# One-core Trainium2 kernel: the convolution's fp32 products and a low-rank projection issued to four column strips of TensorE

## The chip, the cores and the metric

The kernel runs on one core of one Trainium2 chip. The metric is device time in microseconds (us) for one execution. Before the change three runs took 2049.83, 2053.85 and 2056.23 us, a median of 2053.85 us.

## The reference, cut to what matters

The input is `x` with shape (32, 64, 1024), 32 sequences of 64 rows of 1024; four blocks are added to it in turn. Block 0 sees the 64 rows as heads and the 1024 as positions; the others see them as tokens and features.

```python
# block 0: a long convolution along the last axis (u is x, L = 1024)
K = 2.0 * jnp.einsum('hn,hnl->hl', Ct, jnp.exp(P)).real
y = irfft(rfft(u, n=2 * L) * rfft(K, n=2 * L))[..., :L] + u * D[:, None]
x = x + y * mask
# blocks 1 and 2: per-sequence weight chosen by an id
x = x + jnp.einsum('bsi,boi->bso', x, weight[adapter_ids])
# block 3: gated MLP, with rank-16 adapters chosen per sequence
gate = lora_add(x @ W_gate.T, x, A_gate, B_gate)
up = lora_add(x @ W_up.T, x, A_up, B_up)
act = silu(gate) * up
down = act @ W_down.T + SCALE * (act @ A_down[id].T) @ B_down[id].T
x = x + down
```

What is computed here and touched by the change: the causal convolution of each of 64 heads (1024 positions x 32 sequences), and `act @ A_down[id].T`, which gives 16 numbers per token of each sequence, with another `A_down` per sequence.

## The kernel before, in words

Partitions hold 128 positions of the 1024; there are 8 such tiles (`LT`).

**Convolution (L2363 to L2412).** Heads are taken in pairs (`TG` = 2), four pairs to a chunk, eight chunks. Each pair needs a Toeplitz matrix `toep` that SyncE's queue loads from `kpad` in DRAM (1 MB a pair) and the inputs `u` and `urev` (256 KB each), all in rings of four. For each head, `convolve` issues eight fp32 products, one for each distance `d` between output tile and input tile: the stationary operand is a 128x128 block of `toep`, the moving one has (8 - d) x 32 columns, and the output has 128 partitions (the output positions of a tile). All eight add up in one half of a PSUM bank. `conv_done` is raised once per pair; VectorE then masks and adds the pair into `X` (L1479, L1483), and SyncE's queue reloads the ring slot. The last pair is written in three pieces by `convolve_last`. Between chunks `kernels` (L2358) forms the convolution kernel of a later chunk from eight fp32 products whose output has 32 partitions and 32 columns; VectorE and ScalarE prepare its operand `ge`.

**Blocks 1 and 2** follow (from 188 us to about 640 us), and then **block 3** in two stages of 16 sequences. A stage has 22 units of 128 hidden features (unit 0 is half a unit) and then the down projection in panels. In a unit TensorE works off a fixed list: seven sums of Strassen's scheme (`blocks`, F32R, three products per 128x128x512 block: high*high, high*low, low*high), products for the gate and up adapters (`add_ranks`), and `project_down` for the unit before. The F32R type takes fp32 data that was rounded; an exact operand is kept as a high and a low part.

**`project_down` (L2640)** computes the down adapters' projection. `adt` holds, for each of four groups of four sequences, 128 stationary columns: 64 (4 sequences x 16 ranks) of the high part and 64 of the low part. `ahl` holds the activations of the unit as high and low part. For each group the high and then the low activations of its 256 columns are multiplied, so 8 products of 128 output partitions x 256 columns. All sequences of a group meet all adapters of the group; what does not belong together is masked away at the end of the stage. The high half of `adt` and of `ahl` is written by ScalarE (L1031), the low half by VectorE (L1819): `down_ranks_lo`, `v_lo0`, `v_lo1`. At the end of a stage `lift_ranks` (ScalarE) copies the lower 64 output partitions, and VectorE's `down_ranks` adds and masks them.

The order of work on each engine is written out by hand; engines meet at semaphores (`unit_step` counts TensorE's steps of a unit, `evict` VectorE's).

Of the kernel before, what the change touches and what calls it, by code (L numbers as in the profile page):

```python
# [22 lines left out]
P = 128  # L23
# [10 lines left out]
TG = 2  # L34
# [35 lines left out]
LAST_BANKS = (3, 4, 5)  # L70
CHUNK_LINKS = 11
# [14 lines left out]
P1, P6, P2, L11, P5, AD, P7, P4, L21, L22, P3, L12 = range(1, 13)  # L86
USED = (P1, P6, P2, P5, P7, P4, P3)
(V_U2, V_G0, V_SILU0, V_U4, V_U3, V_UP1, V_UP0, V_ACT0, V_RANK1, V_LO0, V_G1, V_SILU1, V_ACT1,
 V_LO1) = range(1, 15)
# [43 lines left out]
def at_step(st, u, e):  # L133
    return u * 12 + (st * (12 * FT + 1) + e)


def emptied(st, u, v):
    return u * 14 + (st * 14 * FT + v)
# [35 lines left out]
def build(nc, ins, out):  # L174
    with ExitStack() as ctx:
# [99 lines left out]
        with placed(0) as s:  # L275
            ahl = sb(s, "ahl", [P, 2, 2, TILE], F32R)
            lt = sb(s, "lt", [P, 3, 2, 2, P], F32R)
            adraw = sb(s, "adraw", [P, SEQ, R])
            adt = sb(s, "adt", [P, GR, P], F32R)
# [148 lines left out]
        ad_lo = sem("ad_lo")  # L428
# [9 lines left out]
        td_lifted = sem("td_lifted")  # L438
        td_added = sem("td_added")
# [28 lines left out]
        def _(sp):  # L468
# [24 lines left out]
            def reload(c, k):  # L493

                q = c * PAIRS + k
                sp.wait_ge(conv_done, q - (RING - 1))
# [137 lines left out]
            def unit(st, u):  # L634

                store_acts(st, u - 1)
                next_ranks(st, u)
                sp.wait_ge(ad_lo, u + st * FT)
                load_down_ranks(st, u)
# [67 lines left out]
            for st in range(NST):  # L707
# [6 lines left out]
                sp.wait_ge(ad_lo, 1 + st * FT)  # L714
# [13 lines left out]
                sp.wait_ge(ad_lo, (st + 1) * FT - 2)  # L728
                load_down_ranks(st, FT - 2)
                store_acts(st, FT - 2)  # L730
                sp.wait_ge(ad_lo, (st + 1) * FT - 1)
# [34 lines left out]
        def _(pool):  # L766
# [46 lines left out]
            def clear(st):  # L813

                pool.memset(ahl[HALF:P].rearrange("p j h w -> p (j h w)").bitcast(F32), 0.0).then_inc(cleared, 1)
                pool.wait_ge(cleared, 2 * st + 1)
                pool.memset(tm[:, 1, 1, SPANS[0][1]:WHOLE_SPANS[0][1]].bitcast(F32), 0.0).then_inc(cleared, 1)
# [59 lines left out]
            for s in range(SEQ):  # L877
                pool.wait_ge(conv_done, 2 * s + 1)
                gather_outer(0, s, slice(0, SPLIT))
# [47 lines left out]
        def _(act):  # L927
# [182 lines left out]
            def down_ranks_hi(st, u, free):  # L1110

                act.wait_ge(adraw_in, u * 16 + (st * FT * 16 + 16))
                act.wait_ge(unit_step, free)
                copy(adt[:, :, 0:HALF].rearrange("p g (s r) -> p g s r", r=R),
                     adraw[:].rearrange("p (g s) r -> p g s r", g=GR)).then_inc(ad_hi, 1)
# [39 lines left out]
            def act_t0(st, u):  # L1155

                act.wait_ge(evict, emptied(st, u, V_ACT0))
                act.wait_ge(unit_step, at_step(st, u, AD))
                copy(ahl[:, 0, 0], s0).then_inc(act_hi, 1)

            def act_t1(st, u):

                act.wait_ge(evict, emptied(st, u, V_ACT1))
                copy(ahl[:, 1, 0], s1).then_inc(act_hi, 1)

            def half_unit(st):
# [3 lines left out]
                act.wait_ge(unit_step, at_step(st, 0, 4))  # L1170
# [3 lines left out]
                act.wait_ge(unit_step, at_step(st, 0, 12))  # L1174
# [3 lines left out]
                down_ranks_hi(st, 0, at_step(st, 0, AD))  # L1178
                act.wait_ge(evict, emptied(st, 0, V_ACT0))
                copy(ahl[0:HALF, 0, 0], s0[0:HALF]).then_inc(act_hi, 1)  # L1180
                act.wait_ge(evict, emptied(st, 0, V_ACT1))
                copy(ahl[0:HALF, 1, 0], s1[0:HALF]).then_inc(act_hi, 1)
# [6 lines left out]
            def unit(st, u):  # L1189

                if not isinstance(u, int):
                    down_ranks_hi(st, u - 1, at_step(st, u - 1, AD))
# [63 lines left out]
            def first_carry(st):  # L1256

                act.wait_ge(evict, emptied(st, FT - 1, V_LO1))
# [34 lines left out]
            def last_unit(st):  # L1293

                u = FT - 1
                down_ranks_hi(st, u - 1, at_step(st, u - 1, AD))
                cut_side_hi(st, 0)
                gate_t0(st, u)
                down_ranks_hi(st, u, at_step(st, u, AD))
# [6 lines left out]

            def lift_ranks(st):

                act.wait_ge(unit_step, at_step(st, FT, 1))
                for j in range(2):  # L1310
                    copy(tmp[HALF:P, j], ps[0:HALF, BANK_AD + j]).then_inc(td_lifted, 1)
# [22 lines left out]
            for st in range(NST):  # L1334
# [24 lines left out]
                for n in range(2, NSIDE):  # L1359
                    panel_hi(st, n)  # L1360
                    if n == 3:
                        lift_ranks(st)
# [9 lines left out]
        def _(dve):  # L1372
# [101 lines left out]
            def add_conv(c, i):  # L1474

                q = c * PAIRS + i
                dve.wait_ge(conv_done, q + 1)
# [245 lines left out]
            def add_last_conv():  # L1723
# [3 lines left out]
                for n, (e, first, end) in enumerate(((0, 0, LT), (1, 0, WK), (1, WK, LT))):  # L1727
                    if first:
                        dve.wait_ge(conv_done, H // TG)
                    else:  # L1730
                        dve.wait_ge(last_parts, n + 1)
# [187 lines left out]
            def v_u2(st, u):  # L1919
                dve.wait_ge(p1_copied, u + st * (FT - 1))  # L1920
# [51 lines left out]

            def v_lo1(st, u):
                dve.wait_ge(act_hi, u * 2 + (st * 2 * FT + 2))
                sub(ahl[:, 1, 1], s1, ahl[:, 1, 0].bitcast(F32)).then_inc(evict, 1)
# [19 lines left out]
            def half_unit(st):  # L1995
# [13 lines left out]
                mul(s1[top], bank(BANK_D)[top], s1[top]).then_inc(evict, 3)  # L2009
# [4 lines left out]
                down_ranks_lo(st, 0)  # L2014
                dve.wait_ge(act_hi, st * 2 * FT + 2)
                sub(ahl[top, 0, 1], s0[top], ahl[top, 0, 0].bitcast(F32))
                sub(ahl[top, 1, 1], s1[top], ahl[top, 1, 0].bitcast(F32)).then_inc(evict, 1)
# [21 lines left out]
                v_lo0(st, 1)  # L2039
# [7 lines left out]
                v_lo1(st, 1)  # L2047
                lo(st, 2, 6)

            def unit(st, u):  # L2050

                down_ranks_lo(st, u - 1)
# [16 lines left out]
                v_lo0(st, u)  # L2069
# [5 lines left out]
                v_lo1(st, u)  # L2075
# [174 lines left out]
            def last_unit(st):  # L2250

                u = FT - 1
                down_ranks_lo(st, u - 1)
# [4 lines left out]
                down_ranks_lo(st, u)  # L2258
# [8 lines left out]
                v_lo0(st, u)  # L2267
# [4 lines left out]
                v_lo1(st, u)  # L2272

            def down_ranks(st):

                blocks = mask[HALF:P, 0:GC].unsqueeze(1).to_broadcast([HALF, 2, GC])
                for j in range(2):
                    dve.wait_ge(td_lifted, 2 * st + j + 1)
                    add(tmp[HALF:P, j], ps[HALF:P, BANK_AD + j], tmp[HALF:P, j]).then_inc(td_added, 1)
                for j in range(2):  # L2280
                    dve.wait_ge(td_added, 2 * st + j + 1)
                    part = tmp[HALF:P, j].rearrange("p (g w) -> p g w", g=2)
                    mul(part, part, blocks).then_inc(td_part, 1)
# [65 lines left out]
        def _(pe):  # L2349
# [12 lines left out]
            def convolve(c, i, first=False):  # L2362
# [7 lines left out]
                for e in range(TG):  # L2370
# [20 lines left out]
            def convolve_last(c, i):  # L2391
# [4 lines left out]
                for n, (e, first, end) in enumerate(((0, 0, LT), (1, 0, WK), (1, WK, LT))):  # L2396
                    rows = urev[:, i % RING, e].rearrange("p l b -> p (l b)")
                    to = ps[:, LAST_BANKS[n], 0:LT * B]
                    for d in range(end):
                        l = max(first, d)  # L2400
                        last = mm(to[:, l * B:end * B], lhsT=toep[:, i % RING, e, d * P:(d + 1) * P],
                                  rhs=rows[:, (l - d) * B:(end - d) * B], start=d == 0, stop=d == end - 1)
                    last.then_inc(conv_done if first else last_parts, 1)
# [210 lines left out]
            def half_unit(st):  # L2614
# [23 lines left out]
                add_ranks(BANK_D, 1, 1, True).then_inc(unit_step, 8)  # L2638

            def project_down(st, u):  # L2640

                pe.wait_ge(ad_lo, u + (st * FT + 1))
                pe.wait_ge(evict, emptied(st, u, V_LO1))
                first = isinstance(u, int) and u == 0
                end = isinstance(u, int) and u == FT - 1
                for g in range(GR):
                    j, cols = g // 2, slice(g % 2 * GC, (g % 2 + 1) * GC)
                    to = ps[:, BANK_AD + j, cols]
                    mm(to, lhsT=adt[:, g], rhs=ahl[:, j, 0, cols], start=first and g % 2 == 0, stop=False)  # L2649
                    last = mm(to, lhsT=adt[:, g], rhs=ahl[:, j, 1, cols], start=False, stop=end and g % 2 == 1)  # L2650
                last.then_inc(unit_step, 1)
# [94 lines left out]
            def down(st):  # L2746
# [4 lines left out]
                pe.wait_ge(td_added, 2 * st + 2)  # L2751
# [88 lines left out]
```

## Time and profile before

| | before |
|---|---|
| median of three runs | 2053.85 us |
| the profiled execution | 2051.15 us |
| its span | 2049.5 us |
| granted TensorE clock, mean | 0.999 |
| TensorE busy | 2003.6 us (98%) |
| VectorE busy | 1771.9 us (86%) |
| ScalarE busy | 1007.3 us (49%) |
| DMA, mean rate | 230 GB/s |

Matmul records (PE) and weight-load records (PEld) are listed apart. An fp32 product shows as two weight loads and two matmul records, an F32R product as one of each. The duration of a matmul record holds its way through the array too; records of the same engine overlap, so what one costs in a row of many is the distance from start to start. L12 is line 12 of the kernel.

### The profile page before, as it was taken

How to read it: one execution, taken by the hardware profiler on the slowest of the kernel's cores; microseconds unless marked ns; L12 is line 12 of the kernel's file. 1: busy time of each engine (PE TensorE's matmuls, PEld its weight loads, DVE VectorE, ACT ScalarE, POOL GpSimd, SP SyncE). 2: the span in 40 equal slices, each digit the busy share in tenths (PEclk: the TensorE clock that was granted, in tenths of full speed). 3: DMA queues.
4: the chain of work that ended last, by engine and by line, in shares of the span. 5: the costliest groups of instructions: out<-in, count | busy, mean ns of one | idle time of the engine just before them, and what ended most of it. 6: DMA issues, size and time to landing. Idle time of an engine off the chain costs nothing.

```text
span 2049.5 us, 34188 instructions
## 1 busy us (share of the span) xinstructions
PE 2003.6 (98%) x10048; PEld 1701.1 (83%) x10048; DVE 1771.9 (86%) x2240; ACT 1007.3 (49%) x1259; POOL 145.0 (7%) x241
## 2 busy tenths in 40 slices
PE   4999999999999999999999999999999999999998
PEld 3999888888888788888888888888888888888887
DVE  7897999999999988888887779989888888868787
ACT  2223888888886543343443434464343443434332
POOL 3200000000003222210000020000000000000000
PEclk9999999999999999999999999999999999999999
DMA  7997999999998667754344996645344344478565
GB/s 282 372 343 295 356 347 354 363 350 361 347 361 329 178 184 210 209 166 123 107 118 145 337 303 212 211 149 143 109 123 120 107 119 113 118 240 303 194 203 190
DMA packets 263681, 471.07 MB, mean 230 GB/s; under 512 B 115462, under 2 KB 119750, under 8 KB 243910
## 3 DMA queue, kind: packets, MB, share of 16 engines
q1 hardware_dynamic: 246498, 427.58, 61.4%
q0 software_dynamic: 14944, 42.50, 6.7%
q8 instruction: 30, 0.49, 0.1%
q10 hardware_dynamic: 2180, 0.26, 0.1%
q14 instruction: 29, 0.24, 0.0%
HBM read 430.10 MB, written 63.73 MB: 241 GB/s over the span
## 4 chain that ended last, share of the span: by engine, by line
PE 85%; DVE 7%; DMA 4%; issue 2%; ACT 1%; DVEq 1%; ACTq 0%; SPq 0%
PE ps L2514 20%; PE ps L2516 19%; PE ps L2515 19%; PE ps L2376 6%; PE ps L2421 5%; PE ps L2423 5%; PE ps L2422 5%; DMA W<-in_w 3%; PE ps L2610 3%; DVE part L1708 1%; PE ps L2430 1%; PE ps L2650 1%; PE ps L2649 1%; DVE rows L1819 1%; ACT part L964 1%
## 5 line engine op out<-in xcount | busy, mean ns | idle before, releaser
L2514 PE MATMUL ps<-rows,oph 128*128 128x512 f32 x1196 | 468.4, 392 | 2.4 <-DVE opl L1819 1.6
L2516 PE MATMUL ps<-rows,opl 128*128 128x512 f32 x1196 | 466.1, 390 | 0.0
L2515 PE MATMUL ps<-rows,oph 128*128 128x512 f32 x1196 | 465.7, 389 | 0.0
L1708 DVE TENSOR_TENSOR part<-W,part 128x2048 fp32r<-128x2048 f32 x152 | 343.0, 2285 | 10.4 <-ACT part L964 9.8
L1822 DVE TENSOR_TENSOR tmp<-ps,tmp 128x512 f32<-128x512 f32 (+2 forms) x344 | 242.7, 706 | 101.8 <-PE ps L2516 53.1
L964 ACT ACTIVATE part<-W 128x2048 fp32r<-128x2048 f32 x152 | 290.9, 1916 | 78.4 <-DMA W<-in_w 56.6
L2516 PEld LDWEIGHTS ps<-rows,opl 128*128 128x128 f32 x1196 | 224.5, 188 | 49.2
L2514 PEld LDWEIGHTS ps<-rows,oph 128*128 128x128 f32 x1196 | 225.3, 188 | 44.3 <-DVE opl L1819 3.6
L2515 PEld LDWEIGHTS ps<-rows,oph 128*128 128x128 f32 x1196 | 224.8, 188 | 40.6
L2514 PE MATMUL ps<-th,wdh 128*128 128x512 f32 (+1 forms) x656 | 249.4, 380 | 2.3 <-DVE tmp L1822 1.2
L2515 PE MATMUL ps<-tl,wdh 128*128 128x512 f32 (+1 forms) x656 | 248.6, 379 | 0.0
L2516 PE MATMUL ps<-th,wdl 128*128 128x512 f32 (+1 forms) x656 | 248.5, 379 | 0.0
L1031 ACT ACTIVATE oph<-sraw 128x512 fp32r<-128x512 f32 x168 | 105.0, 627 | 274.1 <-PE ps L2516 137.5
L2421 PE MATMUL ps<-part,rh 128*128 128x512 f32 x596 | 235.4, 395 | 0.6 <-DVE part L1708 0.3
L2423 PE MATMUL ps<-part,rl 128*128 128x512 f32 x596 | 232.2, 390 | 0.0
L2422 PE MATMUL ps<-part,rh 128*128 128x512 f32 x596 | 232.1, 390 | 0.0
L2376 PE MATMUL ps<-urev,toep 128*128 128x256 f32 x992 | 146.4, 310 | 7.0 <-issue 6.9
L1031 ACT ACTIVATE wdh<-wraw 128x1024 fp32r<-128x1024 f32 (+1 forms) x66 | 66.5, 1008 | 173.3 <-PE ps L2516 169.7
L2376 PEld LDWEIGHTS ps<-urev,toep 128*128 128x128 f32 x992 | 142.1, 193 | 11.0 <-issue 7.0
L2514 PEld LDWEIGHTS ps<-th,wdh 128*128 128x128 f32 x656 | 123.4, 188 | 28.0 <-issue 2.5
L2516 PEld LDWEIGHTS ps<-th,wdl 128*128 128x128 f32 x656 | 123.4, 188 | 23.4
L2515 PEld LDWEIGHTS ps<-tl,wdh 128*128 128x128 f32 x656 | 123.4, 188 | 22.7
(284 smaller groups left out, 2951.0 us busy)
## 6 DMA issues: line engine op xcount, KB each, us to landing
W<-in_w SPq DMA_DIRECT2D x152, 1024.0 KB, 6.8
raw<-in_wgu SPq DMA_DIRECT2D x168, 256.0 KB, 3.1
traw<-kept_acts SPq DMA_DIRECT2D x78, 512.0 KB, 5.0
wraw<-in_wd SPq DMA_DIRECT2D x70, 512.0 KB
toep<-kpad SPq DMA_DIRECT2D x31, 1024.0 KB, 9.7
kept_acts<-tmp SPq DMA_DIRECT2D x84, 256.0 KB, 2.4
lraw<-picked_b SPq DMA_DIRECT2D x176, 96.0 KB, 2.1
lraw<-picked_b SPq DMA_DIRECT2D x176, 64.0 KB, 1.8
```

Source lines behind the costliest of these rows:

```text
L964: nc.scalar.activation(wh[c][:], W[:, c], ACT.Copy).then_inc(w_hi, 1)
L1031: return nc.scalar.activation(to, src, ACT.Copy)
L1708: V.tensor_tensor(out=wl[c][:], in0=W[:, c], in1=wh[c][:].bitcast(F32), op=ALU.subtract).then_inc(w_lo, 1)
L1822: return V.tensor_tensor(out=to, in0=a, in1=b, op=ALU.add)
L2376: last = mm(ps[:, i % RING, (e + 1) * LT * B - n:(e + 1) * LT * B], lhsT=toep[:, i % RING, e, d * P:(d + 1) * P], rhs=rows[:, 0:n], start= ...
L2421: mm(bank(o), lhsT=rh[:, at], rhs=wh[c][:, k], start=first, stop=False)
L2422: mm(bank(o), lhsT=rh[:, at], rhs=wl[c][:, k], start=False, stop=False)
L2423: last = mm(bank(o), lhsT=rl[:, at], rhs=wh[c][:, k], start=False, stop=end)
L2514: mm(to, lhsT=wh, rhs=mh, start=start, stop=False)
L2515: mm(to, lhsT=wh, rhs=ml, start=False, stop=False)
L2516: return mm(to, lhsT=wl, rhs=mh, start=False, stop=stop)
L2610: last = mm(ps[:, to, a:b], lhsT=lt[:, k, j, c], rhs=tm[:, j, c, at + a:at + b], start=start and k == 0, stop=stop and k == 2)
```

## The change

It does four things.

1. Each convolution product is issued as four, one for each strip `t` of 32 output positions: 32 stationary columns of the same `toep` block, the same moving columns, output partitions 32t to 32t + 31. `conv_done` and `last_parts` are raised by the last product of each strip, so they count four per pair, and their waits are multiplied by four.
2. `project_down` is done in fp32, without high and low parts: for each half `j` of the 16 sequences, four products, each of two sequences: 32 stationary columns (2 x 16 ranks), output partitions 32t to 32t + 31, moving columns the 128 of those two sequences (in unit 0 all 512 columns, which also sets the whole bank).
3. So `v_lo0`, `v_lo1`, `down_ranks_lo` and `lift_ranks` are gone; `down_ranks` masks straight from PSUM. ScalarE's copies stay (`act_in`, `adt`, now plain fp32).
4. TensorE's step `AD` is now counted by its own semaphore `ad_done` (four per unit), and `project_down` waits for ScalarE's copies only.

```diff
 def convolve(c, i, first=False):
...
                     for d in range(LT):
                         n = (LT - d) * B
-                        last = mm(ps[:, i % RING, (e + 1) * LT * B - n:(e + 1) * LT * B],
-                                  lhsT=toep[:, i % RING, e, d * P:(d + 1) * P], rhs=rows[:, 0:n],
-                                  start=d == 0, stop=d == LT - 1)
-                last.then_inc(conv_done, 1)
+                        for t in range(STRIPS):
+                            strip = slice(t * SW, (t + 1) * SW)
+                            last = mm(ps[strip, i % RING, (e + 1) * LT * B - n:(e + 1) * LT * B],
+                                      lhsT=toep[:, i % RING, e, d * P + t * SW:d * P + (t + 1) * SW],
+                                      rhs=rows[:, 0:n], start=d == 0, stop=d == LT - 1)
+                            if e == TG - 1 and d == LT - 1:
+                                last.then_inc(conv_done, 1)
...
             def project_down(st, u):
 
-                pe.wait_ge(ad_lo, u + (st * FT + 1))
-                pe.wait_ge(evict, emptied(st, u, V_LO1))
+                pe.wait_ge(ad_hi, u + (st * FT + 1))
+                pe.wait_ge(act_hi, u * 2 + (st * 2 * FT + 2))
...
-                for g in range(GR):
-                    j, cols = g // 2, slice(g % 2 * GC, (g % 2 + 1) * GC)
-                    to = ps[:, BANK_AD + j, cols]
-                    mm(to, lhsT=adt[:, g], rhs=ahl[:, j, 0, cols], start=first and g % 2 == 0, stop=False)
-                    last = mm(to, lhsT=adt[:, g], rhs=ahl[:, j, 1, cols], start=False, stop=end and g % 2 == 1)
-                last.then_inc(unit_step, 1)
+                for j in range(2):
+                    for t in range(STRIPS):
+                        s0 = j * TB + 2 * t
+                        cols = slice(0, TILE) if first else slice(t * P, (t + 1) * P)
+                        last = mm(ps[t * SW:(t + 1) * SW, BANK_AD + j, cols],
+                                  lhsT=adt[:, s0:s0 + 2].rearrange("p s r -> p (s r)"),
+                                  rhs=act_in[:, j, cols], start=first, stop=end)
+                        if j == 1:
+                            last.then_inc(ad_done, 1)
...
-            def down_ranks_lo(st, u):
-
-                dve.wait_ge(ad_hi, u + (st * FT + 1))
-                sub(adt[:, :, HALF:P].rearrange("p g (s r) -> p g s r", r=R),
-                    adraw[:].rearrange("p (g s) r -> p g s r", g=GR),
-                    adt[:, :, 0:HALF].bitcast(F32).rearrange("p g (s r) -> p g s r", r=R)).then_inc(ad_lo, 1)
...
-            def v_lo0(st, u):
-                dve.wait_ge(act_hi, u * 2 + (st * 2 * FT + 1))
-                sub(ahl[:, 0, 1], s0, ahl[:, 0, 0].bitcast(F32)).then_inc(evict, 1)
```

How TensorE's list reads at these places. First the products of one head in the convolution (stationary `toep`, moving `urev`, rows give the output's partitions x columns), before:

```order
L2376 MATMUL ps<-urev,toep 128x256
L2376 MATMUL ps<-urev,toep 128x224
L2376 MATMUL ps<-urev,toep 128x192
L2376 MATMUL ps<-urev,toep 128x160
L2376 MATMUL ps<-urev,toep 128x128
L2376 MATMUL ps<-urev,toep 128x96
L2376 MATMUL ps<-urev,toep 128x64
L2376 MATMUL ps<-urev,toep 128x32
```

and in the changed kernel, where each line stands for four products, one per strip:

```order
L2347 MATMUL ps<-urev,toep 32x256 x4
L2347 MATMUL ps<-urev,toep 32x224 x4
L2347 MATMUL ps<-urev,toep 32x192 x4
L2347 MATMUL ps<-urev,toep 32x160 x4
L2347 MATMUL ps<-urev,toep 32x128 x4
L2347 MATMUL ps<-urev,toep 32x96 x4
L2347 MATMUL ps<-urev,toep 32x64 x4
L2347 MATMUL ps<-urev,toep 32x32 x4
```

Nothing else moved there; neighbours in the list now write different strips. Second, `project_down` between its neighbours, here in the down panels after the last unit (within the units it stands between two F32R blocks in the same way), before:

```order
L2516 MATMUL ps<-th,wdl 128x512
L2649 MATMUL ps<-ahl,adt 128x256
L2650 MATMUL ps<-ahl,adt 128x256
L2649 MATMUL ps<-ahl,adt 128x256
L2650 MATMUL ps<-ahl,adt 128x256
L2649 MATMUL ps<-ahl,adt 128x256
L2650 MATMUL ps<-ahl,adt 128x256
L2649 MATMUL ps<-ahl,adt 128x256
L2650 MATMUL ps<-ahl,adt 128x256
L2514 MATMUL ps<-th,wdh 128x512
```

and in the changed kernel:

```order
L2491 MATMUL ps<-th,wdl 128x512
L2625 MATMUL ps<-act_in,adt 32x128 x8
L2489 MATMUL ps<-th,wdh 128x512
```

The place in the list is the same; eight products stay eight, of a quarter of the partitions and half the columns, in fp32.

## Rows read from the trace of the kernel before

**Rows 1.** Page, parts 1 and 4: busy time, and the chain that ended last.

```profile
PE 2003.6 (98%) x10048; PEld 1701.1 (83%) x10048; DVE 1771.9 (86%) x2240; ACT 1007.3 (49%) x1259; POOL 145.0 (7%) x241
...
PE 85%; DVE 7%; DMA 4%; issue 2%; ACT 1%; DVEq 1%; ACTq 0%; SPq 0%
```

**Rows 2.** Timeline of TensorE, convolution: start us, us, engine line operation, count.

```profile
54.66 18.59 PE L2376 MATMUL ps<-urev,toep 128*128 128x256 f32 x128
73.18 0.69 PE L2358 MATMUL ps<-ge 128*32 128x32 f32 x16
73.88 18.58 PE L2376 MATMUL ps<-urev,toep 128*128 128x256 f32 x128
```

**Rows 3.** Groups of TensorE by form, convolution: count, busy us, mean ns, idle before.

```profile
L2376 PE MATMUL ps<-urev,toep 128*128 128x224 f32 x124 | 34.0, 356 | 0.0
L2376 PE MATMUL ps<-urev,toep 128*128 128x128 f32 x124 | 24.1, 276 | 0.0
L2376 PE MATMUL ps<-urev,toep 128*128 128x32 f32 x124 | 22.5, 264 | 0.0
L2376 PE MATMUL ps<-urev,toep 128*128 128x96 f32 x124 | 22.5, 264 | 0.0
```

**Rows 4.** Timeline at the change from convolution to `kernels`, matmuls, then weight loads.

```profile
37.69 0.56 PE L2376 MATMUL ps<-urev,toep 128*128 128x64 f32 x4
38.18 0.69 PE L2358 MATMUL ps<-ge 128*32 128x32 f32 x16
38.80 0.48 PE L2376 MATMUL ps<-urev,toep 128*128 128x256 f32 x1
...
38.18 0.58 PEld L2358 LDWEIGHTS ps<-ge 128*32 128x32 f32 x16
```

**Rows 5.** Stretches: us, busy (count) of PE, PEld, DVE, ACT, POOL, clock, DMA share, GB/s.

```profile
54.00:73.20 19.20, 19.16 (x145) 18.66 (x145) 14.06 (x26) 4.51 (x6) 5.39 (x10) 1.00 0.90 323
...
sum 77.00, DVE 71.84; mean DVE 17.96
...
150.20:188.00 37.80, 37.80 (x282) 36.95 (x281) 24.08 (x35) 4.72 (x5) 2.39 (x4) 1.00 0.91 337
```

**Rows 6.** Stretch of 2.23 us within one head, TensorE alone: length, busy, clock, DMA share, GB/s.

```profile
90.07:91.70 1.63, 1.63 (x11) 1.00 1.01 415
91.70:92.29 0.59, 0.59 (x8) 1.00 1.06 417
```

**Rows 7.** Timeline of TensorE around one `project_down`.

```profile
710.23 0.39 PE L2516 MATMUL ps<-rows,opl 128*128 128x512 f32 x1
710.46 0.28 PE L2649 MATMUL ps<-ahl,adt 128*128 128x256 f32 x1
710.57 0.28 PE L2650 MATMUL ps<-ahl,adt 128*128 128x256 f32 x1
...
711.29 0.28 PE L2650 MATMUL ps<-ahl,adt 128*128 128x256 f32 x1
711.41 0.40 PE L2514 MATMUL ps<-rows,oph 128*128 128x512 f32 x1
```

**Rows 8.** One unit of block 3 as a stretch (columns as in rows 5).

```profile
796.57:818.07 21.49, 21.49 (x105) 18.12 (x104) 18.26 (x29) 8.79 (x15) 5.99 (x11) 1.00 0.70 208
```

**Rows 9.** Groups of VectorE from 700 us to the end: the subtractions for `ahl`.

```profile
L1819 DVE TENSOR_TENSOR ahl<-tmp,ahl 128x512 fp32r<-128x512 f32 (+1 forms) x86 | 59.1, 688 | 2.8 <-ACT ahl L1031 1.4
```

**Rows 10.** The longest waits of TensorE from 690 us to the end: total us, times, longest.

```profile
PE ps L2514 <- DVE tmp L1822: 1.2, 2, 0.6
PE ps L2514 <- DVE tl L1819: 1.0, 2, 0.7
```

More of the change, by code:

```diff
@@ L70 @@
 LAST_BANKS = (3, 4, 5)
+STRIPS = 4
+SW = P // STRIPS
 CHUNK_LINKS = 11
@@ L427, in build @@
         ad_hi = sem("ad_hi")
-        ad_lo = sem("ad_lo")
+        ad_done = sem("ad_done")
         sums = sem("sums")
@@ L495, in reload @@
                 q = c * PAIRS + k
-                sp.wait_ge(conv_done, q - (RING - 1))
+                sp.wait_ge(conv_done, q * STRIPS - (RING - 1) * STRIPS)
                 if k == PAIRS:
@@ L877, in _ @@
             for s in range(SEQ):
-                pool.wait_ge(conv_done, 2 * s + 1)
+                pool.wait_ge(conv_done, (2 * s + 1) * STRIPS)
                 gather_outer(0, s, slice(0, SPLIT))
@@ L1108, in ranks_hi, with down_ranks_in @@
                 copy(lt[:], lraw[:]).then_inc(lt_hi, 1)
-            def down_ranks_hi(st, u, free):
+            def down_ranks_in(st, u):
                 act.wait_ge(adraw_in, u * 16 + (st * FT * 16 + 16))
-                act.wait_ge(unit_step, free)
-                copy(adt[:, :, 0:HALF].rearrange("p g (s r) -> p g s r", r=R),
-                     adraw[:].rearrange("p (g s) r -> p g s r", g=GR)).then_inc(ad_hi, 1)
+                if st or not isinstance(u, int) or u > 0:
+                    act.wait_ge(ad_done, strips_done(st, u))
+                copy(adt[:], adraw[:]).then_inc(ad_hi, 1)
             def hi(st, u, i):
@@ L1305, in last_unit @@
                 act_t1(st, u)
[L1307 to L1311, printed above, removed]
             group_hi_of(0)
@@ L1476, in add_conv @@
                 q = c * PAIRS + i
-                dve.wait_ge(conv_done, q + 1)
+                dve.wait_ge(conv_done, q * STRIPS + STRIPS)
                 mi = masked[:, i % 2].rearrange("p e l b -> p e (l b)")
@@ L1728, in add_last_conv @@
                     if first:
-                        dve.wait_ge(conv_done, H // TG)
+                        dve.wait_ge(conv_done, H // TG * STRIPS)
                     else:
-                        dve.wait_ge(last_parts, n + 1)
+                        dve.wait_ge(last_parts, (n + 1) * STRIPS)
                     done = ps[:, LAST_BANKS[n], 0:LT * B].rearrange("p (l b) -> p l b", l=LT)[:, first:end]
@@ L2068, in unit @@
                 lo(st, u + 1, 5)
-                v_lo0(st, u)
                 v_g1(st, u)
@@ L2271, in last_unit @@
                 v_act1(st, u)
-                v_lo1(st, u)
             def down_ranks(st):
-                blocks = mask[HALF:P, 0:GC].unsqueeze(1).to_broadcast([HALF, 2, GC])
+                blocks = mask[HALF:P, 0:GC]
+                dve.wait_ge(ad_done, strips_done(st, FT))
                 for j in range(2):
[L2278 to L2283, printed above, removed]
+                    for g in range(2):
+                        cols = slice(g * GC, (g + 1) * GC)
+                        ins_ = mul(tmp[HALF:P, j, cols], ps[g * HALF:(g + 1) * HALF, BANK_AD + j, cols], blocks)
+                    ins_.then_inc(td_part, 1)
             dve.wait_ge(w_lo, base * WC + WC)
@@ L2397, in convolve_last @@
                     rows = urev[:, i % RING, e].rearrange("p l b -> p (l b)")
-                    to = ps[:, LAST_BANKS[n], 0:LT * B]
                     for d in range(end):
                         l = max(first, d)
-                        last = mm(to[:, l * B:end * B], lhsT=toep[:, i % RING, e, d * P:(d + 1) * P],
-                                  rhs=rows[:, (l - d) * B:(end - d) * B], start=d == 0, stop=d == end - 1)
-                    last.then_inc(conv_done if first else last_parts, 1)
+                        for t in range(STRIPS):
+                            strip = slice(t * SW, (t + 1) * SW)
+                            last = mm(ps[strip, LAST_BANKS[n], l * B:end * B],
+                                      lhsT=toep[:, i % RING, e, d * P + t * SW:d * P + (t + 1) * SW],
+                                      rhs=rows[:, (l - d) * B:(end - d) * B], start=d == 0, stop=d == end - 1)
+                            if d == end - 1:
+                                last.then_inc(conv_done if first else last_parts, 1)
             for c in range(NCHUNK - AHEAD, NCHUNK):
```

77 lines of the change are left out of this document (32 added, 45 removed).

## The prediction

> **What bounds the kernel now.** I read the page first, then TensorE's timeline and groups by form, then stretches, and last the waits. TensorE is busy 98% of the span, and the chain that ended last lies on it for 85% [rows 1]. So what the change does to TensorE's own list counts nearly one to one, wherever TensorE has no cover over it. In the convolution its records stand without a gap from 54 to 188 us: eight heads take 18.58 us, and the next chunk starts 19.22 us after the one before [rows 2]. One head is thus 2.30 us (a mid-chunk stretch agrees: 1.63 + 0.59 us and one record more [rows 6]). In block 3 a unit takes 21.49 us, all of it TensorE busy, with VectorE at 18.26 [rows 8], and the longest waits of TensorE after 690 us sum to about 1 us each [rows 10]. VectorE is no bound there, so the removed subtractions save nothing by themselves.
>
> **What a record costs.** Every width has 124 records for 62 heads [rows 3], so an fp32 product is two records, each with a weight load. From 224 to 128 columns the duration falls from 356 to 276 ns, 0.83 ns per column; below 128 it stops falling, 264 ns at 96 and at 32 columns alike [rows 3]. There the moving columns no longer set the pace; the load of 128 stationary columns does. The columns of a head sum to 1152 (256 + 224 + ... + 32). Streaming them twice costs 2 x 1152 x 0.83 = 1.92 us; the head takes 2.30. So 0.38 us per head, 24 us over 64 heads, is the load of weights that short products cannot hide. A load of 32 columns is cheaper: 16 of them in `kernels` span 0.58 us, of which the last one's duration is about 0.11, so one per 0.031 us [rows 4].
>
> **The convolution, changed.** Four products of 32 partitions replace one of 128: the same columns stream four times, with a quarter of the weights each. Everything hangs on how far products in different strips overlap; no row shows it, as the only strip work of the kernel before, `kernels`, uses one strip. The bounds from rows: complete overlap gives the streaming time alone, 1.92 us per head, I take 1.97 with some loss; no overlap at all gives eight records per distance, 8 x (0.83 x 1152 ns, with 0.031 us as the least for 32 columns) = 7.8 us per head. I take overlap: the four products have no operand or output partition in common that one must wait for, except the moving rows, which are only read. TensorE could then give back 0.33 x 64 = 21 us. But other bounds are near. From 54 to 150 us VectorE is busy 14.06 + 71.84 = 85.9 of 96.2 us (the second is its sum over 73.2 to 150.2 us) [rows 5], which leaves 10.3 us; the 40 heads of that stretch would ask for 13. From 150.2 to 188 us VectorE has room (24.08 of 37.80), and DMA moves 337 GB/s at a share of 0.91 [rows 5], against 415 at a share of 1.01 when it is full [rows 6]: 37.8 x 337 / 415 = 30.7 us, room for the 5.5 us that 17 heads would give. So at most 16 us; with DMA near its ceiling, a slot's reload behind the freed slot, and waits that appear when two engines are level, I take **-10 us**.
>
> **The changes of mode.** From convolution to `kernels`: the last short group ends at 38.25 by its 264 ns, so that record began at 37.98, and `kernels` starts at 38.18, 0.20 later instead of about 0.11 [rows 4]. Back: 38.18 to 38.80 is 0.62 us for 16 records of 0.031 (0.50) [rows 4], 0.12 more, of which I count 0.10. So about 0.1 us each way when TensorE goes between 128 and 32 columns. The 15 changes around `kernels` vanish: **-1.4 us**. Each of the 44 `project_down` now gets two: +0.2 us each, counted below.
>
> **`project_down`, changed.** Before: 710.46 to 711.41, 0.95 us, eight records at 0.12 [rows 7]. After: eight fp32 products of 128 columns, 16 records. With overlap, the four strips of a half take 2 x 128 x 0.83 = 0.21 us, both halves 0.43; 16 loads at 0.031 one after another take 0.50, and I take that, plus 0.2 for the changes of mode: 0.70. So -0.25 us in 42 units, -10.5 us. In unit 0 of each stage the products are 512 wide: 2 x 2 x 0.83 x 512 = 1.7 + 0.2 us, +0.95 twice, +1.9. Together **-8.6 us**, all on the path, since a unit is TensorE's time alone. No overlap: 16 x 0.106 + 0.2 - 0.95 = +0.95 us per unit, +40, and +12 for the wide ones.
>
> **The rest.** VectorE loses 86 subtractions of 0.69 us [rows 9] and 44 short ones, under cover of TensorE [rows 8]; nothing. If that cover went (TensorE faster by 3 us per unit), they would count. ScalarE's copies stay. `project_down` waits one engine earlier than before, behind it nothing new queues. The extra raises of `conv_done` and `ad_done` I put at nothing. The removed lift sits between panels, whose waits sum to 1 us [rows 10].
>
> Sum: -10 - 1.4 - 8.6 = -20 us against the profiled execution's 2051.15 (span 2049.5), 2031. That execution lies 2.7 us under the median of the runs, so I forecast **2034 us**.
>
> **A rule against it.** The Trainium skill (TensorE: Matmul & The Clock Gate, Packing small matmuls) says that matmuls start and end strictly in program order, and that three column tiles with 512 moving columns ran 2.38 times as fast; the same page has loads overlap running matmuls only for different row groups, which strips of the same 128 rows are not. No row here shows strips side by side. On the loads the trace disagrees already: loads run under matmuls of the same rows (PEld busy 1701 beside PE 2004 us [rows 1]). What the order rule would do here is the second rival.
>
> **The rivals.**
> 1. *Records start one per 0.031 us, whatever the strip.* For: that is the pace in `kernels` [rows 4], on one strip. Then a distance takes at least 8 x 0.031 = 0.25 us, which binds at 128 columns and fewer. The wide four (832 columns) stream 2 x 0.83 x 832 ns = 1.38 us, the narrow four take 1.0: 2.39 us per head, +0.09 x 64 = +6. With -10 from the other two terms that is -4: 2050 us, no change that counts.
> 2. *The second record of a product holds up the strips behind it (ends slower).* An fp32 product's two records use the same strip [rows 3]. If the second one waits at the head of the list until the first has streamed, then only it and the next strip's first record overlap. A head costs 4 x 1152 x 0.83 = 3.8, with 0.063 as the least for a product 4.0 us: +1.71 x 64 = +109. `project_down`: 8 x 0.106 + 0.2 = 1.05, +0.1 in 42 units (+4), in the wide ones 8 x 0.42 + 0.2 - 0.95 = +2.6 twice (+5). Less 1.4: +117, **2171 us**. It decides if a strip cannot hold one record in waiting. Against it: overlap of neighbours is then still seen. The order rule of the Trainium skill above is what would make it so.
> 3. *No overlap.* (7.8 - 2.3) x 64 + 52 - 1.4 = +403, 2457 us. For: in `kernels` every start lies behind the one before; against: only one strip is used there.
> 4. Something else, either way.
>
> **Chances.** Overlap 0.48; first rival 0.12; second 0.26; third 0.10; other 0.04. "Same" is within 0.3% (6 us), about what a measurement of this kernel can tell from no change. Of the forecast's 0.48, 0.03 falls within it (VectorE or DMA take all): faster 0.46, same 0.13 (with most of rival 1), slower 0.41. The likeliest case alone runs from 2018 (-16, -1.4 and strips' loads side by side, -0.32 x 42) to 2048. The range has to take in rival 2, up to 2180, and leaves rival 3 and the odd case out: 2018 to 2180.
>
> **What would show it.** Right: in TensorE's timeline a chunk's convolution takes 16 to 17.5 us instead of 18.58, with small waits for VectorE or DMA; starts of strips t and t + 1 lie far closer than their streaming time; a unit takes 21.25 us; granted clock stays at 1.00 (2.4 GHz). Rival 1: a chunk at 19, a unit at 21.25. Rival 2: a chunk near 32 us, a unit at 21.6. Rival 3: a chunk near 62 us, a unit at 22.4. The forecast is wrong if a chunk exceeds 18.6 us.

## The result, and the profile after

The changed kernel takes 2058.44 us (median of 20 runs, 2055.24 to 2063.47) against 2053.57 us for the kernel before in 20 runs beside it: ratio 1.0029, 95% interval 1.0023 to 1.0035. That is 5 us slower, right at the bound of 0.3%; the forecast was 20 us faster. The profiled execution has a span of 2054.8 us, 5.3 more than before.

From the profile page of the changed kernel, part 1 and the instruction queue of part 3 (packets, MB, share):

```profile
PE 1986.0 (97%) x13496; PEld 1642.7 (80%) x13496; DVE 1704.9 (83%) x2108; ACT 1009.1 (49%) x1255; POOL 142.5 (7%) x241
...
q8 instruction: 42, 0.69, 0.1%
```

TensorE is busy 17.6 us less than before [rows 1], with a third more records, and still the span is longer. The queue q8 carries instructions, in pieces of 16 KB; before, the same line had 30 packets and 0.49 MB.

TensorE's timeline in the convolution, changed kernel (start us, us, engine line operation, count, idle before with what ended it):

```profile
51.41 2.22 PE L2347 MATMUL ps<-urev,toep 128*32 128x32 f32 x67 [2.91 <-issue]
53.69 0.66 PE L2327 MATMUL ps<-ge 128*32 128x32 f32 x15
...
57.42 4.13 PE L2347 MATMUL ps<-urev,toep 128*32 128x96 f32 x127 [1.25 <-issue]
63.75 8.06 PE L2347 MATMUL ps<-urev,toep 128*32 128x96 f32 x254 [2.19 <-issue]
74.21 2.51 PE L2347 MATMUL ps<-urev,toep 128*32 128x128 f32 x87 [2.41 <-issue]
...
77.37 15.93 PE L2347 MATMUL ps<-urev,toep 128*32 128x256 f32 x512 [0.16 <-issue]
96.21 0.69 PE L2327 MATMUL ps<-ge 128*32 128x32 f32 x16 [2.91 <-DVE ge L1462]
96.96 17.59 PE L2347 MATMUL ps<-urev,toep 128*32 128x256 f32 x512
116.21 0.69 PE L2327 MATMUL ps<-ge 128*32 128x32 f32 x16 [1.66 <-DVE ge L1462]
116.96 15.93 PE L2347 MATMUL ps<-urev,toep 128*32 128x256 f32 x512
...
172.46 5.97 PE L2347 MATMUL ps<-urev,toep 128*32 128x192 f32 x128 [2.73 <-issue]
178.70 4.31 PE L2347 MATMUL ps<-urev,toep 128*32 128x192 f32 x127 [0.26 <-issue]
...
199.43 2.09 PE L2422 MATMUL ps<-part,rh 128*128 128x512 f32 x8 [0.82 <-ACT rh L986]
```

Read three things. First, eight heads in 15.93 us, 1.99 per head, where [rows 2] had 18.58: the strips do overlap. Second, idle put down to "issue", in the middle of a head, where the list has no semaphore; many of the stretches between the gaps have 127, 128 or 254 records. Third, waits for VectorE's `ge` at the end of each chunk in the loop. Blocks 1 and 2 begin at 199.43 us; before, their first product was at 188.24, so the convolution lost 11.2 us:

```profile
188.24 2.09 PE L2447 MATMUL ps<-part,rh 128*128 128x512 f32 x8
```

TensorE's waits from 32 to 200 us (total us, times, longest), changed kernel, and then before:

```profile
PE ps L2347 <- issue: 17.3, 11, 2.9
PE ps L2327 <- DVE ge L1462: 8.0, 4, 2.9
```

```profile
PE ps L2358 <- DVE ge L1465: 1.3, 1, 1.3
```

Before, there was none for issue. The stretches of the whole convolution (us, busy and count of PE, PEld, DVE, ACT, POOL, clock, DMA share, GB/s), after, and then before:

```profile
32.00:199.00 167.00, 141.03 (x4236) 121.13 (x4228) 127.17 (x220) 31.57 (x41) 25.66 (x45) 0.97 0.89 323
```

```profile
32.00:188.00 156.00, 154.54 (x1143) 150.22 (x1142) 125.99 (x219) 31.75 (x41) 25.94 (x45) 1.00 0.94 345
```

TensorE works 13.5 us less and stands 24.5 us more: +11. The granted clock is 0.97, not 1.00: three times it fell to its lower level, each time just after a wait. One wait, of 2.91 us, ends at 96.2 us; the stretches that follow it (TensorE at 1.2 GHz where the clock column says 0.50):

```profile
96.20:98.00 1.80, 1.72 (x32) 1.30 (x36) 1.73 (x5) 0.37 (x1) 0.60 (x1) 0.84 1.04 410
98.00:100.00 2.00, 2.00 (x37) 1.61 (x32) 1.93 (x3) 1.28 (x1) 0.00 (x0) 0.50 1.01 404
100.00:102.00 2.00, 2.00 (x56) 1.57 (x52) 1.93 (x3) 0.00 (x0) 0.00 (x0) 0.79 1.05 400
```

That chunk took 17.59 us where its neighbour takes 15.93, so the drop cost 1.7 us, and as much again at 172.46 (5.97 against 4.31 us for 128 records). A third drop follows the gap before 185.74 (0.60 from 185.7 to 190 us). Not every gap has one: after the 2.91 us before 51.41 and the 2.41 before 74.21 the clock stayed at 1.00.

The account of the convolution: eight chunks at 2.65 us less would be 21.2 us, and it ended 11.2 later, so 32.4 us are to be found. Issue took 17.3, the waits for `ge` 6.7 more than before, the two drops of the clock that can be read off 3.3, and a wait for ScalarE at its end 0.8. The other 4 us, with the third drop in them, were not taken apart.

The projection, changed kernel, and one unit as a stretch:

```profile
825.37 0.39 PE L2491 MATMUL ps<-rows,opl 128*128 128x512 f32 x1
825.69 0.64 PE L2625 MATMUL ps<-act_in,adt 128*32 128x128 f32 x16
826.26 0.50 PE L2489 MATMUL ps<-rows,oph 128*128 128x512 f32 x1
826.60 0.40 PE L2490 MATMUL ps<-rows,oph 128*128 128x512 f32 x1
...
804.34:825.69 21.35, 21.35 (x114) 17.46 (x113) 16.75 (x26) 8.90 (x14) 6.48 (x12) 1.00 0.73 204
```

Against [rows 7] and [rows 8], a unit is 0.14 us shorter. Sixteen records take from 825.69 to 826.26, 0.57 us, instead of 0.95; but the first one starts 0.32 after its wide neighbour instead of 0.23 (0.09 more), and the second wide record after it comes 0.34 us later, where 0.23 is the pace of such records: 0.11 more. Together that is 0.18 us less, of which the unit shows 0.14. Narrowing to 825.80 to 825.815 us shows four records in flight:

```profile
825.69 0.32 PE L2625 MATMUL ps<-act_in,adt 128*32 128x128 f32 x4
```

Each lasts 0.30 us and all four together 0.32, so they started within 0.02 us of each other.

The balance: +11.2 at the start of blocks 1 and 2, +10.6 at the first projection (694.98 against 684.41 us), +5.5 after the 22 of stage 0, +4.0 after those of stage 1, +5.3 at the end. Block 3 gave back 5.3 us net. It won 2.1 us between the first two calls of the projection and 5.9 in the 40 units that follow the second call of either stage; it lost 1.0 at the wide projection of stage 1, 0.4 between the stages and 1.3 after the last call. The convolution took 11.2.

### The profile page after: what moved, and what is told of

It reads as the page before. It is cut to its first block, busy times and chain, and to the rows that moved or that the text cites. A ratio compares the mean times of both kernels' runs of the same rounds, so it can differ in the third digit from the quotient of the medians.

```text
span 2054.8 us, 40994 instructions
## 1 busy us (share of the span) xinstructions
PE 1986.0 (97%) x13496; PEld 1642.7 (80%) x13496; DVE 1704.9 (83%) x2108; ACT 1009.1 (49%) x1255; POOL 142.5 (7%) x241
## 3 DMA queue, kind: packets, MB, share of 16 engines
q10 hardware_dynamic: 2180, 0.26, 0.1%
## 4 chain that ended last, share of the span: by engine, by line
PE 85%; DVE 9%; issue 3%; DMA 2%; ACT 1%; SPq 0%; DVEq 0%; ACTq 0%
PE ps L2489 19%; PE ps L2490 19%; PE ps L2491 19%; PE ps L2396 6%; PE ps L2398 6%; PE ps L2397 6%; PE ps L2347 3%; PE ps L2585 3%; PE ps L2405 2%; PE ps L2625 1%; DVE rows L1816 1%; DVE X L1480 1%; DVE masked L1476 1%; DMA traw<-kept_acts 1%; DVE rraw L1816 1%
## 5 line engine op out<-in xcount | busy, mean ns | idle before, releaser
L1819 DVE TENSOR_TENSOR tmp<-ps,tmp 128x512 f32<-128x512 f32 (+1 forms) x340 | 240.3, 707 | 165.0 <-PE ps L2491 89.0
L2491 PEld LDWEIGHTS ps<-rows,opl 128*128 128x128 f32 x1196 | 224.5, 188 | 50.1
L2347 PE MATMUL ps<-urev,toep 128*32 128x256 f32 (+7 forms) x3968 | 134.1, 296 | 24.6 <-issue 24.4
L2347 PEld LDWEIGHTS ps<-urev,toep 128*32 128x32 f32 x3968 | 114.1, 114 | 44.2 <-issue 28.9
```

Of the source, the lines that this page charges most:

```text
L1819: return V.tensor_tensor(out=to, in0=a, in1=b, op=ALU.add)
L2347: last = mm(ps[strip, i % RING, (e + 1) * LT * B - n:(e + 1) * LT * B], lhsT=toep[:, i % RING, e, d * P + t * SW:d * P + (t + 1) * SW], rh ...
L2491: return mm(to, lhsT=wl, rhs=mh, start=False, stop=stop)
```

## The experiments

The question after the first look: what is the idle put down to issue? Theory F: TensorE's code, which comes in pieces and arrives too late. Each product of a head became four, so a pair has 256 instructions (64 products, each two loads and two matmuls) instead of 64. The 12 pieces more on q8 were there to be explained too, and 128 records between two gaps are 256 instructions with their loads. Ten kernels ran.

### Each part alone

`e1_projection_only` keeps the convolution's whole products:

```diff
-                        for t in range(STRIPS):
...
+                        last = mm(ps[:, i % RING, (e + 1) * LT * B - n:(e + 1) * LT * B],
+                                  lhsT=toep[:, i % RING, e, d * P:(d + 1) * P], rhs=rows[:, 0:n],
+                                  start=d == 0, stop=d == LT - 1)
+                last.then_inc(conv_done, STRIPS)
```

> The projection in strips, the convolution as before (whole products, conv_done raised by four at once). Both theories: units 21.35 us as in the changed kernel instead of 21.49, blocks 1 and 2 starting at 188 us as before; 2051 - 6 = about 2047 us, ratio 0.997. If the projection's strips disturbed something outside their own unit, the ratio would be 1.000 or above.

Measured: 2047.22 us, ratio 0.9975 (0.9962 to 0.9988); blocks 1 and 2 start at 188.71 us. As expected: this part alone is a gain.

`e2_conv_only` is the kernel before with `convolve` and `convolve_last` of the change.

> The convolution in strips, the projection as before. Theory F (TensorE's straight-line code arrives too late): blocks 1 and 2 start near 199 us as in the changed kernel, units 21.49, total about +11 us, ratio 1.005. Rival V (VectorE's slower preparation of ge in this build, by whatever reason lies in the other part of the change): the start would be near 190 us and the ratio about 1.000.

Measured: 2065.09 us, ratio 1.0066 (1.0053 to 1.0080), blocks 1 and 2 at 198.12 us, 13.3 us of idle by issue and 10.6 by `ge` after the first product. The loss is the convolution's alone; rival V, a slower VectorE by reason of the other part, fell. The two parts add up to +0.4%, near the 1.0029 of both.

### The loop written out

`e3_unrolled`, and the same edit in the kernel before as `e4_before_unrolled`:

```diff
-            with pe.Fori(1, NCHUNK - AHEAD) as c:
+            for c in range(1, NCHUNK - AHEAD):
```

> The changed kernel with the loop over chunks 1 to 5 written out, so that no code is run twice: 16 more pairs are read for the first time. Theory F: idle of TensorE put down to issue in the convolution grows from 17 us (after the first product) to 30 to 40 us, in all chunks and not only in the first and last; about 16 more pieces on the instruction queue q8; ratio to the kernel before 1.008 to 1.015. Rival D (the stalls come from the data: toeplitz loads, PSUM or SBUF taken by others) : no change against the changed kernel, 1.003.

> Control: the kernel before with the same loop written out, 4 KB of TensorE code per pair instead of 16. Theory F: about 4 to 5 more pieces on q8, no issue idle worth naming, 1.000 +- 0.001. If writing out the loop costs by itself (register work, something else), it shows here as well.

Measured: e3 2079.37 us, ratio 1.0141 (1.0125 to 1.0157); e4 2055.05 us, 1.0014 (1.0004 to 1.0023). In e3 blocks 1 and 2 start at 219.56 us. The waits of TensorE and the instruction queue from 33 to 219 us in e3, from after the first product to the end of the convolution:

```profile
PE ps L2347 <- issue: 34.1, 22, 3.5
PE ps L2327 <- issue: 3.4, 1, 3.4
...
q8 instruction: 33, 0.54, 1.1%
```

and the queue in the changed kernel from 32 to 199 us:

```profile
q8 instruction: 16, 0.26, 0.6%
```

(4 pieces in the kernel before up to 188 us, 9 in e4.) The products, their operands and their order on the data are those of the changed kernel; only code that was run from the loop four more times is now read anew. The 16 pairs of those four passes brought 17 pieces more, TensorE stands 37.5 us for issue instead of 17.3, and the convolution ends 20.1 us later than in the changed kernel, nearly the same 20.2. The gaps, before absent from the loop's later passes, stand in every chunk (3.24 us in chunk 0, 2.62 in the first of the loop, then 2.02, 1.56, 2.05 and so on). Rival D, in which the data alone is at fault, fell. In e4, at a quarter of the code per pair, no gap by issue appears after the first product; its 0.14% is not explained by gaps on TensorE.

How a gap goes: in the changed kernel TensorE stood from 48.5 to 51.41 us. Stretches of that gap, first, and the instruction queue in the middle one:

```profile
48.50:49.10 0.60, 0.00 (x1) 0.00 (x0) 0.55 (x2) 0.00 (x0) 0.00 (x0) 1.00 0.84 256
49.10:50.10 1.00, 0.00 (x0) 0.00 (x0) 0.97 (x3) 0.47 (x1) 0.08 (x1) 1.00 0.96 342
50.10:51.40 1.30, 0.00 (x0) 0.00 (x0) 1.16 (x3) 0.47 (x2) 1.02 (x2) 1.00 1.05 411
```

```profile
q8 instruction: 1, 0.02, 5.5%
```

The piece moved between 49.1 and 50.1 us and in neither neighbour. So its transfer began only after the engine had stopped, and work went on 1.4 us after it ended.

The other gaps go the same way. The changed kernel's convolution has ten gaps by issue of 0.26 us or more after the first product, and in the trace every one ends 1.2 to 1.6 us after a piece on q8 has landed. In the four longest (2.41 to 2.91 us) the piece began to move 0.2 to 0.7 us after TensorE had stopped, in the other six before that. Six more pieces moved without such a gap.

### Quieter DMA queues

`e8_half_reloads` moves only half of each reload of `toep`; from the fifth pair on the other half keeps old values, so that much of the output is not the reference's.

```diff
-                load_toeplitz(q, k % RING)
+                load_half_toeplitz(q, k % RING)
```

> The changed kernel with only half of each Toeplitz reload moved (from the fifth pair on the upper half of the columns is left as it was), so DMA has some 30% less to do in the convolution. Rival C (the code waits behind full DMA queues): the stalls shrink to half or less and blocks 1 and 2 start at 190 us or before. Theory L (a piece of code is asked for only when the engine is nearly out of it, and takes some 2.4 us whatever the load): the stalls stay at 0.3 to 3 us each, 10 or more of them, 13 to 17 us in all.

Measured: 2046.23 us, ratio 0.9963 (0.9952 to 0.9975); blocks 1 and 2 at 189.65 us; DMA 252 GB/s from 32 to 189 us. Still 17 pieces, but:

```profile
PE ps L2353 <- issue: 8.1, 6, 2.5
```

8.5 us in all with the last product's, against 17.3. Neither theory holds alone: about half of the standing goes with the load on the DMA engines, the rest (single gaps up to 2.5 us) does not. One piece takes 0.9 to 1.1 us here and 0.9 to 1.25 in the changed kernel, so the transfer itself is not what shrank; what decides when a piece starts to move, no run shows.

### Strips only where the code is run again

`e5_strips_in_loop`: projection in strips, convolution in strips in the loop, whole products in chunk 0 and the last eight pairs.

> Strips for the projection and for the convolution of chunks 1 to 5 (the loop, whose code is read once and run five times); whole products in chunk 0 and in the last eight pairs. Theory F (TensorE's code arrives too late): issue idle only in the first pass of the loop, about 4 stalls and 6 us; passes 2 to 5 take VectorE's 18.3 us per chunk instead of 19.2 and wait 1.5 to 3 us for ge; blocks 1 and 2 start between 188 and 192 us; ratio 0.997 to 0.999, so no better than the projection alone. Rival D (strips disturb the data traffic in every pass): the stalls also stand in passes 2 to 5, ratio above 1.000.

Measured: 2050.85 us, ratio 0.9988 (0.9978 to 0.9998). Chunks in the loop:

```profile
64.03 8.06 PE L2347 MATMUL ps<-urev,toep 128*32 128x96 f32 x254 [1.07 <-issue]
75.31 4.18 PE L2347 MATMUL ps<-urev,toep 128*32 128x128 f32 x87 [3.23 <-issue]
...
98.95 0.77 PE L2327 MATMUL ps<-ge 128*32 128x32 f32 x16 [2.97 <-DVE ge L1462]
99.70 17.43 PE L2347 MATMUL ps<-urev,toep 128*32 128x256 f32 x512
118.73 0.69 PE L2327 MATMUL ps<-ge 128*32 128x32 f32 x16 [1.61 <-DVE ge L1462]
119.53 17.59 PE L2347 MATMUL ps<-urev,toep 128*32 128x256 f32 x512
```

Issue idle in the first pass only, as F says (4.3 us in two gaps rather than 6 in four). But a later chunk takes 18.5 to 20.0 us from one `kernels` to the next, not 18.3, and blocks 1 and 2 start at 195.20, which is 7.0 us later than before and outside what was expected. What the strips save, TensorE waits for `ge`, and two of the chunks run 1.5 to 1.7 us longer at a lower clock (0.50 from 120 to 122 us, after a wait of 1.61). Even in the passes where its code was at hand, the convolution gained nothing.

### Half as many strips

`e7_two_strips`: the convolution in two strips of 64 positions, the projection as in the change.

```diff
+HALVES = 2
+HW = P // HALVES
...
-                        for t in range(STRIPS):
-                            strip = slice(t * SW, (t + 1) * SW)
+                        for t in range(HALVES):
+                            strip = slice(t * HW, (t + 1) * HW)
```

> The convolution in two strips of 64 output positions, the projection in four as in the changed kernel. 8 KB of TensorE code per pair instead of 16. Theory F: half as many pieces on q8 in the convolution (about 9 to 10 instead of 17), and a pair takes 4 us per 8 KB, so a piece is wanted every 8 us and the stalls shrink to under 6 us in all. If two strips overlap as four do, a head takes 1.95 to 2.1 us; blocks 1 and 2 start near 188 to 192 us; ratio 0.997 to 1.000. If two strips do not overlap, a head takes 3.9 us.

Measured: 2044.07 us, ratio 0.9958 (0.9945 to 0.9971), the lowest median of the kernels with the reference's result (its interval overlaps that of e1, so the two are not told apart by the time alone; the trace has the convolution 3.1 us shorter). 9 pieces on q8, no gap by issue over 0.1 us after the first product:

```profile
93.08 0.69 PE L2329 MATMUL ps<-ge 128*32 128x32 f32 x16 [1.71 <-DVE ge L1464]
93.83 16.38 PE L2349 MATMUL ps<-urev,toep 128*64 128x256 f32 x256
...
167.12 8.29 PE L2349 MATMUL ps<-urev,toep 128*64 128x256 f32 x128 [1.52 <-DMA u<-in_u]
...
185.18 2.09 PE L2424 MATMUL ps<-part,rh 128*128 128x512 f32 x8 [0.63 <-ACT rh L988]
```

16.38 us for eight heads, nearly the 15.93 of four strips, at half the code. Blocks 1 and 2 start 3.1 us earlier than before; 10.5 us of waits for `ge` and 2.3 us for DMA take most of the rest of 17.6 us (8 x 2.2), and the first chunk in the loop took 17.46 us at a lower clock (0.72 from 54 to 60 us) after a wait of 3.15. The four chunks after it as one stretch (columns as above), and all of VectorE's waits in it:

```profile
74.09:148.61 74.52, 68.38 (x1088) 59.70 (x1089) 71.40 (x127) 18.05 (x24) 9.85 (x16) 1.00 0.99 366
...
DVE masked L1478 <- PE ps L2349: 0.2, 1, 0.2
```

VectorE is busy 71.40 of 74.52 us and waits once, for 0.2 us. So the chunk of 18.6 us is VectorE's, and TensorE's wait for `ge` is what it has left over.

### How far TensorE looks ahead

`e6_strip_outermost`: the loop over strips outside the one over distances, the same products in another order.

> The changed kernel with the loop over strips outside the loop over distances: the eight products of a strip follow one another, the next strip's come 8 products (32 instructions with their loads) later. If TensorE starts records only in the order of the list, or looks ahead by a few instructions, strips overlap hardly at all: a head takes up to 7.8 us, a chunk 62 us, in all up to +350 us. If it looks far ahead (32 instructions or more), a head stays at 2 to 2.3 us. I expect the first: ratio 1.15 to 1.18.

Measured: 2351.02 us, ratio 1.1451 (1.1428 to 1.1473), and a chunk:

```profile
92.45 58.43 PE L2347 MATMUL ps<-urev,toep 128*32 128x256 f32 x509
```

7.3 us per head. So neighbours in the list overlap, and the overlap does not reach over eight products. At this pace no gap by issue appears after the first product either: 16 KB of code are wanted every 15 us.

### The changes of mode

`e9_split_projection` puts the second half of each projection one block later.

```diff
+                project_down(st, u - 1, (0,))
...
+                project_down(st, u - 1, (1,))
```

> The changed kernel with the projection cut in two: the first half of the sequences at its place, the second half one block (12 wide F32R products) later. Nothing is added but one more change into and out of the strip mode per unit, 42 units. If each pair of changes costs what the gap rows of the changed kernel show (0.09 in, 0.19 out, 0.28 us together), a unit takes 21.35 + 0.28 = 21.63 us and the total is +12 us against the changed kernel, ratio 1.009. If the smaller gain of the projection has another cause than the changes of mode, a unit stays under 21.45 and the ratio at 1.003 to 1.005.

Measured: 2071.14 us, ratio 1.0096 (1.0080 to 1.0112). The projections of two units:

```profile
827.62 0.42 PE L2625 MATMUL ps<-act_in,adt 128*32 128x128 f32 x8
830.93 0.43 PE L2625 MATMUL ps<-act_in,adt 128*32 128x128 f32 x8
849.31 0.42 PE L2625 MATMUL ps<-act_in,adt 128*32 128x128 f32 x8
```

A unit is 21.69 us, +0.34 for one more pair of changes. The whole projection now takes 0.77 us (0.57 and the 0.20 beside it), so 0.34 of that goes to entering and leaving the strips.

### Taking the wait for ge away

`e10_kernels_later` starts from e7 and issues `kernels` one pair later, after the first pair of the next chunk.

```diff
-            kernels(AHEAD)
...
-                kernels(c + AHEAD)
+                    if i == 0:
+                        kernels(c + 1)
```

> Two strips of 64 in the convolution as in e7, and TensorE's products for the convolution kernel of a later chunk (kernels) one pair later in its list, after the first pair of the next chunk. Theory V (TensorE stands at the end of each chunk for VectorE's ge, 1.1 to 3.2 us each, only because of the place in its list): these waits vanish, chunks take 17.1 to 18 us, blocks 1 and 2 start at 178 to 182 us, ratio 0.992 to 0.995. Rival M (VectorE and DMA are full anyway, or the Toeplitz loads then come later): new waits for toep or u appear and the start stays at 184 to 188 us, ratio 0.996 to 0.998.

Measured: 2055.04 us, ratio 1.0014 (1.0004 to 1.0025), 11 us worse than e7. Waits of TensorE and then of VectorE, 32 to 205 us:

```profile
PE ps L2349 <- DMA u<-in_u: 19.6, 9, 4.3
...
PE ps L2329 <- DVE ge L1464: 1.2, 1, 1.2
```

```profile
DVE ksb L1470 <- ACT ksb L954: 24.9, 5, 7.4
```

The waits for `ge` went but for one of 1.2 us, and VectorE now stood for the copy behind `kernels`, after which `kpad` and with it the Toeplitz loads and the inputs queued behind them came late; blocks 1 and 2 start at 200.82 us. Theory V of this run (the place in TensorE's list alone) fell. Rival M had the new waits right and their size wrong, as it left the start at 184 to 188. The wait for `ge` was the mildest place for a bound that lies in VectorE. Whether VectorE's own order could be changed was not tried.

## Why the prediction was wrong, point by point

- **Strips overlap (0.48 given): right.** 1.99 us per head, where 1.97 was taken; the second rival (second record blocks the strips behind it) and the third (no overlap) fell. I had said the first rival, one record per 0.031 us, would bind narrow products; starts come closer than that.
- **The order rule of the Trainium skill** (TensorE: Matmul & The Clock Gate, Packing small matmuls: matmuls start and end strictly in program order). In the projection four records start within 0.02 us, the next four 0.11 us after the last of them, and the four that raise `ad_done`, one per product, are the last four to start. So the second record of the first product starts after the first record of the fourth. If a product's two records stand side by side in the instruction list, which no view here prints, the trace does not agree with the rule for neighbours in different strips; e6 shows that the freedom is short.
- **The step that failed:** "The extra raises of `conv_done` and `ad_done` I put at nothing" stood where all side costs of four times as many instructions should have been counted. I priced records and never code. The missing term is the supply of TensorE's code, 16 KB per pair where it is first run: 17.3 us of standing. It follows the code (e3 and e4: 20.2 us more standing for 17 pieces more, none at a quarter of the code; e7: none at half), and about half of it goes with the load on the DMA engines (e8). The profile page before had what was needed: a packet on q8 for 16 KB, and pairs outside the loop (12 of 32) against 4.6 us a pair.
- **The cap by VectorE was named but too generous.** I took -10 of 21 us. In e7, without gaps by issue, the convolution gained 3.1; in e5 it lost 7.0. Of the 10.3 us that I saw left on VectorE from 54 to 150 us, 5.1 lay in the first chunk [rows 5], and that chunk got longer in e7 (20.0 us); the four after it went from 19.2 us only to between 18.2 and 19.0, where VectorE was busy 96% and waited once, for 0.2 us.
- **A cost not thought of:** after three of the waits the granted clock fell to 1.2 GHz, 1.7 us each where it could be read off. I had expected it to stay at 1.00.
- **The projection, -8.6 us:** e1 measured 2053.15 - 2047.22 = -5.9. Per unit -0.14 instead of -0.25. The changes of mode cost 0.34 (e9), not 0.2; the records between them took 0.43 (four groups of four, 0.11 us apart), not the 0.50 I took. That makes 0.77 in place of 0.70, and 0.04 of the miss has no place. The wide projection of stage 1 cost 1.0, as forecast (0.95). VectorE's removed subtractions were put at nothing; the 2.1 us won between the first two calls of stage 0, in spite of the wider first projection, are not TensorE's own work and may be theirs. No run took that apart.
- **The changes around `kernels`, -1.4 us:** e6, where nothing waits there, agrees. `kernels` starts at 47.73 us among the last records of the convolution, and the next record of the convolution comes 0.53 us later instead of 0.62.
- **Sums:** the lower bound of 2018 does not come out of its terms (2054 - 16 - 1.4 - 13.4 + 1.9 is 2025); from 150 to 188 us there are 16 heads, not 17 (5.3 us instead of 5.5); and without overlap a head adds up to 7.7 us, not 7.8 (e6 took 7.3). None of these changes the forecast.
- **Range and chances:** 2058.44 lies in the range of 2018 to 2180, but that range held it for rival 2's sake, which is not what happened. "Same" had 0.13, for VectorE and DMA taking all of the gain, or for rival 1. VectorE did take most of it (e7), but what turned a small gain into a loss is in neither.

## What to carry to other kernels

Count instructions as bytes: splitting a product multiplies the engine's code. Here straight-line code of 16 KB in 4 us stood for its own supply, the more so with full DMA queues, and 16 KB in 8 us (e7) did not. Split only as far as pays (two strips gave nearly all that four gave), and rather inside loops that run again. And before speeding up one engine where two are level, find who waits for whom in a round: a saving becomes a wait elsewhere, and here waits of 1.6 to 2.9 us sometimes cost clock on top.

## What the runs showed of the hardware that I had not expected

- fp32 products in neighbouring column strips run fully side by side: four starts within 0.02 us, eight heads in 15.93 us.
- TensorE's code comes in pieces of 16 KB on q8. Ten of the 16 in the changed kernel's convolution went with a gap of 0.3 to 2.9 us, which ended 1.2 to 1.6 us after the piece had landed; four of them moved only after the engine had stopped.
- Entering and leaving a strip mode costs 0.34 us a pair between 512-column products (e9).
- After some waits of 1.6 to 2.9 us the clock was at 1.2 GHz for a while, at a cost of 1.5 to 1.7 us; after others of the same length it was not (2.91 us before 51.41 us, and 1.66 before 116.21).
